# Two low-part flags, a reordered base split and filler matmuls in the last tile of a transformer block kernel

## The reference

```python
x = x + attn(layernorm(x))             # x: 2 x 2048 x 1024, float32
x = x + ffn(layernorm(x))
# attn: per token (b, s), over its 32 heads of 32 values
q, k, v = (h @ w.T + b for each)       # wq, wk, wv rounded to fp8 e4m3, then float32
scores = einsum('bshd,bstd->bsht', q, k) / sqrt(32)
context = einsum('bsht,bstd->bshd', softmax(scores), v)
# ffn: base layer plus the two best of eight experts' rank-16 updates
result = x @ base_w.T + base_b + 2.0 * lora(top2(softmax over gate logits))
```

## Time and profile before

| | |
|---|---|
| median of 3 runs (lowest, highest) | 1324.54 us (1323.55, 1327.37) |
| the profiled execution | 1322.41 us, of which the span is 1320.6 us |
| busy share of the span | PE 97%, DVE 84%, ACT 51%, PEld 51%, POOL 21% |
| mean granted PE clock | 0.994 |
| the chain that ended last | PE 91%, DVE 5%, DMA 1%, ACT 1%, issue 1% |
| HBM traffic | 66 GB/s over the span |
| tile 1 begins on PE (first product of k) | 86.38 us |
| tile 2 begins on PE | 134.26 us |
| tile 3 begins on PE | 172.7 us |

### The profile page before, as it was taken

How to read it: one execution, slowest core, us unless ns; L and a number is a source line. 1 busy time by engine, 2 the same in 40 slices (tenths; PEclk the granted TensorE clock), 3 DMA queues, 4 the chain that set the end, 5 groups by cost and what they waited for, 6 DMA issues and landing times.

```text
span 1320.6 us, 30261 instructions
## 1 busy us (share of the span) xinstructions
PE 1279.1 (97%) x12476; PEld 678.5 (51%) x12476; DVE 1104.4 (84%) x1569; ACT 674.7 (51%) x1033; POOL 277.3 (21%) x305
## 2 busy tenths in 40 slices
PE   6888999999999999999999999999999999999996
PEld 4554555555555455555545555554555555455543
DVE  5898888888888888888888888888888888888884
ACT  4864455555445555544555554445555444555530
POOL 0202211212221121222112122211212221121220
PEclk9999999999999999999999999999999999999998
DMA  9723332222222222222322212332221233222110
GB/s 366 257 65 81 82 79 58 69 55 56 79 79 79 60 68 57 56 78 79 79 60 67 60 57 74 79 79 62 66 62 59 70 80 79 63 64 63 46 35 33
DMA packets 162011, 103.72 MB, mean 79 GB/s; under 512 B 135616, under 2 KB 136640, under 8 KB 161984
## 3 DMA queue, kind: packets, MB, share of 16 engines
q1 hardware_dynamic: 161984, 103.36, 27.8%
HBM read 69.78 MB, written 16.78 MB: 66 GB/s over the span
## 4 chain that ended last, share of the span: by engine, by line
PE 91%; DVE 5%; DMA 1%; ACT 1%; issue 1%; SPq 0%; POOL 0%; DVEq 0%
PE dense_acc L1408 24%; PE acc L1268 24%; PE acc L1277 24%; PE attn_ps L1361 7%; PE dense_acc L1416 4%; PE attn_ps L1369 2%; DMA work<-wT_dram 1%; PE low_ps L1392 1%; PE low_ps L1391 1%; PE low_ps L1393 1%; PE dense_acc L1431 1%; DVE base_parts L856 1%; PE dense_acc L1299 1%; ACT work L360 1%; PE acc L1310 0%
## 5 line engine op out<-in xcount | busy, mean ns | idle before, releaser
L1408 PE MATMUL dense_acc<-base_parts,x 128*128 128x512 f16 x1488 | 331.0, 380 | 0.0
L360 ACT COPY work<-work 32x512 f16<-32x512 f16 x384 | 236.0, 614 | 8.6
L1408 PEld LDWEIGHTS dense_acc<-base_parts,x 128*128 128x128 f16 x1488 | 143.4, 98 | 168.0 <-issue 1.8
L951 DVE SCALAR_TENSOR_TENSOR work<-acc,acc_to_a,biases_sb 128x512 f32<-128x512 f32 x192 | 143.7, 750 | 48.0 <-PE acc L1277 45.5
L1268 PE MATMUL acc<-w_hi_k,x_hi 128*128 128x512 f16 x496 | 118.9, 383 | 0.0
L531 POOL TENSOR_TENSOR work<-work 128x1024 f16<-128x1024 f32 x32 | 68.1, 2130 | 240.6 <-ACT work L751 236.7
L1277 PE MATMUL acc<-w_hi_k,x_lo 128*128 128x512 f16 x496 | 117.2, 379 | 0.0
L1277 PE MATMUL acc<-w_hi_q,x_lo 128*128 128x512 f16 x496 | 117.2, 379 | 0.0
L1268 PE MATMUL acc<-v_parts,x_hi 128*128 128x512 f16 x496 | 117.2, 379 | 0.0
L1277 PE MATMUL acc<-v_parts,x_lo 128*128 128x512 f16 x496 | 117.2, 379 | 0.0
L1268 PE MATMUL acc<-w_hi_q,x_hi 128*128 128x512 f16 x496 | 117.1, 379 | 0.0
(11 more groups left out here) (193 smaller groups left out, 2124.4 us busy)
## 6 DMA issues: line engine op xcount, KB each, us to landing
work<-x_dram SPq DMA_DIRECT2D x64, 512.0 KB, 3.6
work<-work SPq DMA_DIRECT2D x256, 64.0 KB, 2.0
work<-x_dram SPq DMA_DIRECT2D x124, 128.0 KB, 3.2
out_dram<-work SPq DMA_DIRECT2D x31, 512.0 KB, 2.9
work<-wT_dram SPq DMA_DIRECT2D x16, 512.0 KB, 9.2
v_parts<-wT_dram SPq DMA_DIRECT2D x8, 512.0 KB, 14.1
base_parts<-wT_dram SPq DMA_DIRECT2D x5, 512.0 KB, 10.4
biases_sb<-bias_dram SPq DMA_DIRECT2D x4, 512.0 KB, 10.4
```

The source lines that it names most:

```text
L360: copy(diag[c * QD:(c + 1) * QD, :, c, j::NQ, :], src).then_inc(vdiag_ready, 1)
L951: nc.vector.scalar_tensor_tensor(out=ev[:, s], in0=acc[bank][:, :], scalar=acc_to_a[:, i:i + 1], in1=bias[g][:, s], op0=ALU.mult, op1=ALU. ...
L1408: nc.tensor.matmul(dense_acc[n][:, :], rows_part[:, k, :], w_part[:, k, cols], start=(k == 0 and m == 0), stop=False)
```

## The change

There are four parts.

1. The flag is split in two. The low parts of k and q have flag 0; those of v have flag 1, with its squares in another accumulator (`v_low_ps`). On DVE the first flag is computed before the first low part of tile 1's input and published after the softmax sum; the flag of v is computed after the turn of the probabilities and published in tile 1. PE loads flag 1 at the first product of v. In tile 1 PE does `spread_flag(1)` after the first half of k, and the context product of tile 0 moves behind the second half.
2. `x2_rows` now stages chunk 1 of the base matrix, and chunks 2 to 6 are in the slots, so that chunk k (from 3 on) waits for chunk k-1. `x2_high` no longer waits for the base matrix.
3. The base chunks move: on DVE chunks 3 and 4 are split in tile 1 before the turn of q, chunk 5 before the turn of v, chunks 6 and 7 around the softmax. ACT's high parts follow, and ACT's row statistics of tile 2 move to the end of tile 0. PE's base product of tile 0 is `dense_first`: six chunks of both halves, then a wait for all eight, then the last two chunks.
4. In the last tile all eight late `spread_v` copies are DVE's. In the tail `finish` of tile 30 goes ahead of `x2_low`, and PE gets 8, 16 and 4 matmuls (`keep_busy`) whose results nobody reads.

```diff
-        SHIFT = 3
+        BASE_FREE = 3
-                  "base": [bias["base"]] + [base_slots[:, SHIFT + i, :] for i in range(KC - SHIFT)]
-                  + [x2_rows, lora_up[:, :]]}
+                  "base": [bias["base"], x2_rows] + [base_slots[:, k, :] for k in range(BASE_FREE, KC)]
+                  + [lora_up[:, :]]}
-        flag_ps = low_ps[:, 2 * P:3 * P]
+        flag_ps = [low_ps[:, 2 * P:3 * P], dense_acc[1][:, 0:P]]
+        v_low_ps = dense_acc[0][:, 0:P]
# ACT high_parts and DVE split, chunk k
-                    if g == "base" and k >= SHIFT:
+                    if g == "base" and k >= BASE_FREE:
-                        act.wait_ge(w_lo_done["base"], k - SHIFT + 2)
+                        act.wait_ge(w_lo_done["base"], k)
# ACT x2_high
-                if isinstance(p, int) and p == 0:
-                    act.wait_ge(w_lo_done["base"], KC - 1)
# DVE
+            def flag_v_low_parts():
+                dve.wait_ge(lo_squared, 2)
+                nc.vector.tensor_reduce(lo_top[:, :], v_low_ps, AX.X, ALU.max,
+                                        apply_absolute_value=True).then_inc(lo_step, 1)
+                dve.wait_ge(lo_step, 3)
+                nc.vector.tensor_scalar(lo_flag[:, :], lo_top[:, :], 0.0, None, ALU.not_equal).then_inc(lo_flagged, 1)
# DVE, last tile
-                for c in C_DVE:
+                for c in C_DVE if nxt else C_ACT_LAST + C_DVE:
                     spread_v(nc.vector.tensor_copy, c)
# DVE, tail
-                x2_low(t - 1)
                 finish(t - 2, 0, x1)
                 finish(t - 2, 1, x1)
+                x2_low(t - 1)
# PE
-                if any_low[0] is None:
-                    pe.wait_ge(flag_ready, 1)
-                    any_low[0] = pe.value_load(lo_flag_int[0:1, 0:1], min_val=0, max_val=1)
-                with pe.If(any_low[0] > 0):
+                if any_low[i] is None:
+                    pe.wait_ge(flag_ready, i + 1)
+                    any_low[i] = pe.value_load(lo_flag_int[0:1, i:i + 1], min_val=0, max_val=1)
+                with pe.If(any_low[i] > 0):
+            def dense_first():
+                pe.wait_ge(w_lo_done["base"], KC - 2)
+                for n in range(NB):
+                    pe.wait_ge(base_free, n + 1)
+                    dense(n, 0, KC - 2)
+                pe.wait_ge(w_lo_done["base"], KC)
+                turn_low(0)
+                for n in range(NB):
+                    dense(n, KC - 2, KC)
+                dense_lora(0)
+            def keep_busy(n):
+                for i in range(n):
+                    nc.tensor.matmul(acc[0][:, :], x_hi[:, i % KC, :], w_hi[FIRST][:, i % KC, 0:HALF], start=True,
+                                     stop=True)
             def tail(t):
+                pe.wait_ge(b_biased, 2 * t)
+                keep_busy(KC)
                 context(t - 1)
                 turn_low(t - 2)
                 dense_lora(t - 2)
+                keep_busy(2 * KC)
                 turn2(t - 1)
+                keep_busy(KC // 2)
```

More of the change, by code:

```diff
@@ L733, in step @@
                     return first_step()
+                one = isinstance(t, int) and t == 1
                 if nxt:
-                    row_statistics(t + 1)
+                    if not one:
+                        row_statistics(t + 1)
                     normalise_quads(t + 1)
@@ L742, in step @@
                 nc.scalar.copy(k_parts[:, 0, :, :], turned3).then_inc(a_hi_ready, 1)
-                if isinstance(t, int) and t == 1:
-                    high_parts("base", w_hi["base"], 6, KC)
+                if one:
+                    high_parts("base", w_hi["base"], 4, 5)
                 x2_high(t - 1)
+                if one:
+                    high_parts("base", w_hi["base"], 5, 6)
                 act.wait_ge(bt_ready, t + 1)
@@ L756, in step @@
                 nc.scalar.copy(v_parts_t[:, :, 0, :], turned3).then_inc(v_hi_ready, 1)
+                if one:
+                    high_parts("base", w_hi["base"], 6, 7)
                 if prev:
@@ L761, in step @@
                 nc.scalar.activation(soft, soft, ACT.Exp, scale=score_undo[:, 0:1]).then_inc(exped, 1)
+                if one:
+                    high_parts("base", w_hi["base"], 7, KC)
                 act.wait_ge(v_lo_ready, t + 1)
@@ L1259, in _ @@
             pe.wait_ge(consts_set, EXPERTS + 4)
-            any_low = [None]
+            any_low = [None, None]
             def project(g, n, bank, done):
+                i = 1 if g == "v" else 0
                 cols = slice(n * HALF, (n + 1) * HALF)
@@ L1346, in square_low_parts @@
                         part = w_lo[g][:, k, c * P:(c + 1) * P]
-                        mm = nc.tensor.matmul(low_ps[:, out_cols], part, part,
-                                              start=(g != "v" and k == first and c == 0),
-                                              stop=(g != SECOND and k == KC - 1 and c == HID // P - 1))
-                if g == "v" and last == KC:
+                        mm = nc.tensor.matmul(dst, part, part, start=(k == first and c == 0),
+                                              stop=(k == KC - 1 and c == HID // P - 1))
+                if g != FIRST:
                     mm.then_inc(lo_squared, 1)
@@ L1502, in step @@
                 project(FIRST, 0, 0, a_acc)
-                context(t - 1)
+                one = isinstance(t, int) and t == 1
+                if one:
+                    spread_flag(1)
+                else:
+                    context(t - 1)
                 pe.wait_ge(v_biased, 2 * t - 1)
                 project(FIRST, 1, 1, a_acc)
+                if one:
+                    context(0)
                 pe.wait_ge(v_biased, 2 * t)
@@ L1528, in step @@
                 attend(scored)
-                pe.wait_ge(w_lo_done["base"], KC)
-                if nxt:
+                if one:
+                    dense_first()
+                elif nxt:
                     dense_all(t - 1)
```

53 lines of the change are left out of this document (30 added, 23 removed).

## The result

| | before | changed |
|---|---|---|
| median of 5 runs (lowest, highest) | 1324.09 us (1323.55, 1327.37) | 1314.87 us (1314.17, 1316.49) |
| the profiled execution, its span | 1322.41, 1320.6 us | 1315.04, 1313.2 us |
| mean granted PE clock | 0.994 | 0.995 |

The ratio of the changed kernel to the one before is 0.9928 (95% interval 0.9913 to 0.9942): it is 9.2 us faster (by the interval 7.7 to 11.5), where 8.2 were forecast (1316.3 us, range 1313.3 to 1320.3).

A forecast was written before the change was run, and what follows sets the result against it. PE, 97% busy, was taken as the bound, so only the front before tile 2 and the tail could pay: 3.9 + 4.3 = 8.2 us, giving 1314.2 us profiled, 1316.3 us as median, range 1313.3 to 1320.3.

The forecast's parts named there:

- The flag's wait counts only as far as DVE is late for it: Tile 1: DVE's list sets the time; DVE reaches chunk 0's split at 88.1 instead of 88.37.
- Splits off the way to q: Tile 1, DVE from chunk 0's split to `x2_low`: three splits and a gap go, 24.12 us becomes 19.6.
- given back later: Tile 1, DVE from turn of q to turn of probabilities: three splits, 3.6 us, come in; 0.8 falls into a wait.
- rival (a): Front: chunks 5, 6, 7 each expose one ACT high part, 1.1 us; 3.3 of 3.9 go, 1319.6 us; chance 16%.
- The LoRA load: Before tile 2: issued once chunk 7 is split, no longer hidden; at 4.5 us tile 2 starts at 130.4, 3.9 earlier.
- the forecast's own bound by tile 2's `x_lo`: End of front: DVE's next step, ending at 129.4, limits the front gain to 4.8 us.
- Rival (c): Before tile 2: unhidden LoRA load is slow, 13.4 us, and the kernel ends slower, 1325.2 us; chance 4%.
- the cover that the prediction had named for its other small costs: Tile 1: PE has 2 to 4 us to spare before the base product, hiding a register load and cold stretch.
- One of its signs of being right: Tile 1: PE would wait about 3 us before the turn of the second norm.
- The tail: After the loop: earlier context, fillers keeping the clock and `finish` ahead of `x2_low` gain 4.3 us.
- Rival (b): Tail: fillers do not hold the clock, turn and product stay cold, 0.5 + 1.2 us less, 1318.0 us; chance 11%.
- the parts named for "faster": Whole kernel, below 1320.5 us: forecast, (a), (b), gain above 10 us and six tenths of (d); 0.89 by count.

The follow-up runs named there:

- flags alone: Kernel before with part 1 only (two flags, tile 0's context behind the second half of k): 1323.41 us, ratio 0.9996.
- both edits, with fillers further on: Changed kernel with ACT's chunk 4 high part ahead of k's, POOL's bias wait moved, ten fillers before tile 1's scores: 1312.65 us, ratio 0.9916.
- both edits: Changed kernel with ACT's chunk 4 high part ahead of k's and POOL's base-bias wait moved to its use: 1312.84 us, ratio 0.9917.

## Why the prediction was right

- *PE is 97% busy, only front and tail can pay.* Right: the loop is 1141.4 us to 0.01 in all profiles but that with the LoRA matrix loaded twice.
- *The flag's wait counts only as far as DVE is late for it.* Right in the kernel before: removing it alone gave 0.3 us. In the changed order the joint flag costs 1.1, since the context then comes late for DVE. The prediction had counted only the 0.27 us by which the split starts earlier.
- *Splits off the way to q, 4.5 us; given back later.* Forecast 19.6 and 18.2 us for the two stretches of DVE, measured 19.44 and 18.52. Counted from the scores of tile 0, chunk 7's split ended within 0.2 us of where forecast: rival (a), exposed high parts, did not happen; DVE waited for ACT once, 1.43 us for a forecast 1.45. Three splits (5, 6, 7) left the way, as the prediction counts; the list of this stretch ahead of it shows two fewer, because chunk 4's came into it from further up.
- *The LoRA load.* This is the mis-sized term. I took 4.5 us from the row of this very transfer; it took 3.3, and 3.1 to 3.3 in the ten other profiles with the changed order. In the kernel before it was issued 0.38 us behind a load of the next tile of the same size; now none has been issued for 11.8 us (timeline of SP, before, then changed):

```profile
117.53 0.33 SPq L463 DMA_DIRECT2D work<-x_dram  x1
117.91 0.43 SPq L471 DMA_DIRECT2D lora_up<-lora_b_dram  x1
...
113.90 0.33 SPq L464 DMA_DIRECT2D work<-x_dram  x1
125.72 0.33 SPq L472 DMA_DIRECT2D lora_up<-lora_b_dram  x1
```

The flags alone kept the neighbour, and took 4.5 again. That the two loads hinder each other is the likely reason; no run changes the neighbour alone. At 3.3 the forecast's own bound by tile 2's `x_lo` holds, a gain of 4.8; 4.58 was measured, and tile 2 did start with `x_lo`. The Trainium skill's fit (DMA: Bandwidth & Descriptors, "Anatomy of one DMA"), which it gives for another issuing engine, came to 3.2 us as an estimate, and the runs agree with it.
- *Rival (c), the load as a risk.* Its mechanism is real (0.21 us of PE waiting, and one for one when doubled), but its price was too low: a wait of 3.27 us also costs 1.19 us of clock behind it.
- *POOL.* I missed that POOL's list had a wait for the base bias ahead of tile 2's row root. The row statistics came earlier (92.9), and POOL began only when the bias landed, at 95.2. The rest of PE's wait is one slow POOL operation, as told above. It cost nothing at the end, as PE had time to spare; this was the cover that the prediction had named for its other small costs. One of its signs of being right was therefore not seen: PE did not wait 3 us before the turn of the second norm. In the profile of the changed kernel it did not wait there at all; in the eight other profiles with the early flag in which POOL held it up by 0.32 us at most, it waited 1.64 to 2.24.
- *The tail.* Forecast 4.3, measured 4.25: the turn came 0.48 us earlier (forecast 0.57), the product started 2.93 earlier (3.07) and was 1.28 shorter (1.2). Taken out one by one, order is worth 2.0, the copies 0.67 (forecast 0.55), the fillers 2.8 (forecast 1.7 by before's trace). That the forecast hits to 0.05 is in part luck: it and the measured 4.25 both start from one profile in which the old tail kept its clock long. From the tail of the flags alone, the same code, the gain is 5.9. Rival (b), fillers that do not hold the clock, is refuted by the granted clock of 1.00. But what the prediction said against it, that short gaps leave the clock, is wrong as a rule: behind 1.76 us in tile 1 it fell.
- *The sum.* 8.2 forecast, 4.58 + 4.25 = 8.83 by the two lengths, 9.2 by the medians. Of the difference 0.7 is the front, where the load was priced too high; the remaining 0.4 lies within the interval. It goes the way that the clocks suggest: the profiled execution of before had 0.994, and of the 30 runs of that kernel beside the experiments 28 had 0.992 or less, which fits an old tail that was as a rule colder than in the trace from which I forecast. No run measures this share. The chances were added up wrongly: the parts named for "faster" come to 0.91, not 0.89.

## What to carry to other kernels

Before a wait of the bound engine is priced, follow who that engine next waits for: here 4.2 us of PE idleness cost 0.3, because the next wait was for DVE, and the way to shorten the stretch was to take operations out of DVE's list ahead of the thing PE needs. Where the bound engine must idle in a tail, fillers that end just before the wait does gave 1.7 to 2.8 us here, and the tails with them agreed to 0.15 us where two without had differed by 1.65. When a load is moved out from under cover, do not price it from a row in which another load was issued just ahead of it. And when an operation is moved forward, look in every engine's list for waits that stand ahead of what it feeds, as POOL's for the bias did here.

## What the runs showed of the hardware

- The granted clock's fall depends on the moment, not only on the length of the wait. The clearest pair is PE's wait before the turn of the second norm in tile 1: behind 2.24 us the turn and the next eight matmuls took 1.09 and 1.89 us in one kernel (both edits, with fillers further on) and 1.45 and 3.26 in another (both edits), with the same code up to there. Likewise, after 2.53 us of idleness before the last context (the kernel before) the next stretch ran at a granted clock of 1.00, and after 2.58 us in the same place (flags alone) at 0.59. After only 1.76 us in tile 1 (changed kernel) eight matmuls took 3.52 us, at 0.57.
- The fall can come after the wait: without fillers the turn behind 3.91 us of idleness was warm (1.09 us), and the product, after a further wait of 1.10 us, took 9.85 us instead of 7.08, at a granted clock of 0.71.
- A load of 512 KB with no other issued just ahead of it took 3.1 to 3.3 us in eleven profiles. It took 4.5 in the two (before, flags alone) where another of the same size was issued 0.4 us before it.
- A POOL operation on 128x1 that took 0.19 us in the other profiles took 1.05 us in one and, on another line, 1.11 in one. The cause is open.
